# Second expert layer in three f16 products, the first bias inside the gelu, and the second layer two blocks behind the first

## What is computed

```python
x = x + attention(layernorm(x), Wq, bq, Wk, bk)        # x [4, 512, 128]
n = layernorm(x)
gate = softmax(n @ w_gate.T)                           # 8 experts
h = gelu(einsum('td,edh->teh', n, W1) + b1)            # W1 [8, 128, 512]
y = einsum('teh,ehd->ted', h, W2) + b2                 # W2 [8, 512, 128]
x = x + einsum('td..', y, top2(gate))                  # two of eight per token
```

## Time and profile before

| | |
|---|---|
| median of 3 runs | 401.67 us (398.6 to 402.32) |
| profiled execution, its own time | 401.8 us |
| its span | 400.1 us |
| TensorE busy | 338.6 us (85%) |
| ScalarE busy | 247.6 us (62%) |
| VectorE busy | 231.2 us (58%) |
| GpSimd busy | 143.0 us (36%) |
| mean granted TensorE clock | 0.978 |
| weights of a block, `wblk<-wpk` x46 | 288.0 KB, 2.7 us to landing |
| slots of a group, `xg<-xs` x10 | 260.0 KB, 3.4 us to landing |

### The profile page before, as it was taken

The page is one execution under the profiler, slowest core; times in us unless marked ns, Lnnn a source line. Parts: engine busy times, 40 slices in busy tenths (PEclk is TensorE's granted clock), DMA queues, the critical chain, the costliest instruction groups (busy, mean ns, idle before and its releaser), DMA issues.

```text
span 400.1 us, 7419 instructions
## 1 busy us (share of the span) xinstructions
PE 338.6 (85%) x2522; PEld 176.3 (44%) x2522; DVE 231.2 (58%) x619; ACT 247.6 (62%) x342; POOL 143.0 (36%) x159
## 2 busy tenths in 40 slices
PE   6777888899978989989989899999889997999900
PEld 2511333323323333323323233235779986998900
DVE  5497788677867987877789987853150000001304
ACT  1407779989878975659875768688464543444400
POOL 4994213211027017013006211036237744453450
PEclk9999999999999999999999999999899999999975
DMA  5979001100001101000201420001345754678214
GB/s 144 326 194 214 12 0 29 26 2 0 28 1 27 29 0 55 0 2 0 53 1 40 153 94 2 0 15 70 116 153 195 241 210 143 215 240 295 82 48 155
DMA packets 32863, 36.11 MB, mean 90 GB/s; under 512 B 3090, under 2 KB 23642, under 8 KB 32828
## 3 DMA queue, kind: packets, MB, share of 16 engines
q1 hardware_dynamic: 30332, 30.49, 25.9%
q0 software_dynamic: 2496, 5.15, 3.9%
HBM read 10.71 MB, written 9.25 MB: 50 GB/s over the span
## 4 chain that ended last, share of the span: by engine, by line
PE 48%; DVE 24%; ACT 9%; issue 7%; DMA 6%; POOL 3%; SPq 1%; POOLq 0%; DVEq 0%; ACTq 0%
DVE q_aug L862 13%; PE AV L1246 10%; PE SM L1199 9%; PE ST L1319 8%; PE ST L1234 6%; DMA xg<-xs 3%; ACT probs L760 2%; DVE q_aug L869 2%; PE ST L1298 2%; PE ST L1303 2%; PE ST L1301 2%; PE ST L1302 2%; DVE stats L816 2%; ACT xn L636 2%; POOL xs L529 2%
## 5 line engine op out<-in xcount | busy, mean ns | idle before, releaser
L862 DVE TENSOR_REDUCE q_aug<-SM 128x1 f16<-128x512 f32 x240 | 153.4, 688 | 46.2 <-PE SM L1199 45.2
L760 ACT ACTIVATE probs<-ST 128x1024 f32<-128x1024 f32 x128 | 125.5, 1022 | 37.3 <-PE ST L1234 36.9
L1199 PE MATMUL SM<-kTm,qT 128*128 128x512 f16 x240 | 84.0, 388 | 15.2 <-DVE q_aug L862 10.0
L1234 PE MATMUL ST<-qT,kTm 128*128 128x512 f16 x256 | 76.2, 383 | 5.0 <-ACT qT L642 4.9
L1246 PE MATMUL AV<-probs,v_aug 128*32 128x512 f32 x512 | 68.2, 605 | 3.1 <-ACT avs L752 2.9
L1199 PEld LDWEIGHTS SM<-kTm,qT 128*128 128x128 f16 x240 | 19.8, 97 | 96.0 <-DVE q_aug L862 86.3
L529 POOL DMA_INDIRECT xs<-x2s,pos x32 | 31.6, 986 | 79.5 <-DVE pos L975 70.9
L539 POOL DMA_INDIRECT yt<-w,dest x46 | 44.8, 973 | 37.5 <-ACT w L673 25.9
L665 ACT ACTIVATE w<-ST 128x512 f32<-128x512 f32 x46 | 27.3, 596 | 48.0 <-PE ST L1303 45.4
L1319 PE MATMUL ST<-w 128*128 x368 | 51.9, 285 | 1.3 <-ACT w L665 1.3
L1319 PEld LDWEIGHTS ST<-w 128*128 128x128 f32 x368 | 45.6, 195 | 1.6 <-issue 1.5
(11 more groups left out here) (174 smaller groups left out, 389.8 us busy)
## 6 DMA issues: line engine op xcount, KB each, us to landing
wblk<-wpk SPq DMA_DIRECT2D x46, 288.0 KB, 2.7
xg<-xs SPq DMA_DIRECT2D x10, 260.0 KB, 3.4
...
```

The lines of the kernel that those rows point to most:

```text
L760: act.activation(probs[:, n % 4, :, :], ST[:, n % 2, :, :], ACT.Exp, scale=SCALE).then_inc(exp_done, 1)
L862: dve.tensor_reduce(q_aug[:, b % 2, m % 4, m // 4, 24:25], SM[m % 2][:, :], AX.X, ALU.max, negate=True).then_inc(sm_max, 1)
L1199: pe.matmul(SM[m % 2][:, :], qT0[:, b % 2, h // 4, P * (m % 4):P * (m % 4) + P], kTm[:, b % 2, h // 4, h % 4, :], start=True, stop=True).t ...
L1234: mm = pe.matmul(ST[:, n % 2, k % 2, :], kTm[:, b % 2, g, k, P * c:P * c + P], qT1[:, g % 2, :], start=True, stop=True)
```

## The change

The second layer's products become f16. W2, scaled by 64, is split into a high part and a rest (`w2pk`) by eight pairs of ScalarE instructions and eight of GpSimd in batches 1 and 2, slots 12 to 15. W2 is loaded from DRAM in batch 1 into the memory of `w1`, instead of at the start into a tile of its own. The hidden values are split per block on VectorE (`split_hidden`: `hh`, `hl`, three buffers each), and `hf` has two buffers. `down` makes 12 f16 products of 128 columns (high by high, high by rest, rest by high) in place of four f32 ones; `take_y` divides by 64. The bias product with `sel` is gone: b1 is loaded as 32 rows beside the gate's, transposed with them, and stored in f32 behind each expert's weights, so a ring entry has 258 KB in place of 288. The gelu reads it as a per-partition bias, in four pieces of 128 columns. So a ring entry is free when the gelu has read it, and `fetch_weights` waits for `gelu_done`. The copy of `xgT` moves from ScalarE to VectorE. LAG is 2, and the router's steps of batch 3 are spread over steps 1 to 10.

```diff
-    WB = 2 * F + P
-    HR = 3
+    WB = 2 * F + 2 * HC
-        LAG = 1
+        LAG = 2
-            jobs = {0: [("out", b, 3)], 2: [("x2", b)], 3: [("lg", b)], 4: [("rk", b)]}.get(i, [])
+            jobs = {0: [("out", b, 3)], 4: [("x2", b)], 6: [("lg", b)], 8: [("rk", b)]}.get(i, [])
...
                 if v >= RW:
-                    sp.wait_ge(up_full, v - RW + 1)
+                    sp.wait_ge(gelu_done, v - RW + 1)
...
             for b in range(B):
                 if b == 1:
+                    sp.wait_ge(s_wl, E)
+                    sp.dma_start(w1[:, :, :].rearrange("p e (c d) -> p e c d", c=HC),
+                                 W2.rearrange("e (c p) d -> p e c d", p=P)).then_inc(s_wf[1], 16)
                     sp.wait_ge(x1_done, G)
...
+            def rest_w2(i):
+
+                pool.wait_ge(s_vh, i + 1)
+                pool.tensor_tensor(w2pk[:, i, F:2 * F], w1[:, i, :], w2pk[:, i, 0:F], ALU.subtract).then_inc(s_vl, 1)
...
             def gelu(v):
 
+                if v == 0:
+                    act.wait_ge(s_vl, E)
                 act.wait_ge(up_full, v + 1)
-                if v >= HR:
-                    act.wait_ge(down_done, v - HR + 1)
-                act.activation(hf[:, v % HR, :], UP[v % 2], ACT.Gelu, scale=1.0 / WSCALE).then_inc(gelu_done, 1)
+                if v >= 2:
+                    act.wait_ge(split_done, v - 1)
+                for c in range(HC):
+                    cs = slice(P * c, P * c + P)
+                    last = act.activation(hf[:, v % 2, cs], UP[v % 2][:, cs], ACT.Gelu, scale=1.0 / WSCALE,
+                                          bias=wblk32[:, v % RW, F + c:F + c + 1])
+                last.then_inc(gelu_done, 1)
...
+            def split_w2(e):
+
+                act.wait_ge(s_wf[1], 16)
+                act.activation(w1[:, e, :], w1[:, e, :], ACT.Copy, scale=WSCALE).then_inc(s_vfs, 1)
+                act.wait_ge(s_vfs, e + 1)
+                act.activation(w2pk[:, e, 0:F], w1[:, e, :], ACT.Copy).then_inc(s_vh, 1)
...
+            def split_hidden(v):
+
+                dve.wait_ge(gelu_done, v + 1)
+                if v >= 3:
+                    dve.wait_ge(down_done, v - 2)
+                link(dve.tensor_copy(hh[:, v % 3, :], hf[:, v % 2, :]))
+                dve.tensor_tensor(hl[:, v % 3, :], hf[:, v % 2, :], hh[:, v % 3, :], ALU.subtract).then_inc(split_done, 1)
...
                     for job in misc_of_step(b, i):
                         empty_misc(job)
-                    if i == 0:
+                    for v in todo[i:i + 1]:
+                        split_hidden(v)
+                    if i == 1:
                         second_stats(b)
...
                 dst, wb = UP[v % 2], wblk[:, v % RW, :]
-                pe.matmul(dst, wb[:, 2 * F:WB], sel[:, :, :].rearrange("p c n -> p (c n)"), start=True, stop=False)
...
-                pe.wait_ge(gelu_done, v + 1)
+                pe.wait_ge(split_done, v + 1)
+                wv = w2pk[:, bass.ds(expert[v], 1), :].rearrange("p a n -> p (a n)")
                 for c in range(HC):
-                    last = pe.matmul(dst, hf[:, v % HR, P * c:P * c + P],
-                                     w2[:, bass.ds(expert[v], 1), P * c:P * c + P].rearrange("p a n -> p (a n)"),
-                                     start=False, stop=(c == HC - 1))
+                    hi, lo = slice(P * c, P * c + P), slice(F + P * c, F + P * c + P)
+                    pe.matmul(dst, hh[:, v % 3, hi], wv[:, hi], start=False, stop=False)
+                    pe.matmul(dst, hh[:, v % 3, hi], wv[:, lo], start=False, stop=False)
+                    last = pe.matmul(dst, hl[:, v % 3, hi], wv[:, hi], start=False, stop=(c == HC - 1))
                 last.then_inc(down_done, 1)
```

117 lines of the change are left out of this document (58 added, 59 removed).

## The result

The changed kernel takes 422.3 us (median of four runs, 420.9 to 423.1) beside 401.5 for the kernel before on the same chip, a ratio of 1.0525 with a 95% interval of 1.0481 to 1.057. A second job gave 422.6 and 1.0556 (1.0500 to 1.0613). The prediction was 412 (398 to 424): the direction and the range held, the amount was half of the 20.8 us measured.

What follows compares the result with a forecast made beforehand. The slots' load loop, not TensorE, was taken to become the bound. 401.8 us plus middle 3.8, tail 3.5, start 2 and clock 1.5, less attention 0.5, gave 412 us, range 398 to 424.

Steps and rivals of the forecast that it cites:

- the attention's term: Attention of the four batches: bias splits go, W2 splits arrive on ScalarE; -0.5 us (-2 to +2).
- TensorE's price of a block, 1.38 us: Expert blocks: cheaper products cut TensorE's 1.89 us to 1.38, saving 23 us over 46 blocks if TensorE stayed the bound.
- The second rival (419): GpSimd and VectorE collide: each split loses 0.5 us to sends, 419 us; chance 0.13 together with register moves.
- The dynamic slices bring nine register moves: Second layer on TensorE: nine register moves instead of five, priced at nothing; high bound 0.6 us a block.
- The fourth rival (419): Register moves pace the second layer's products, 0.6 us more each, 419 us; chance 0.13 together with the collision.
- The slots' loop binds: Middle: the loop through the slots' load becomes the bound; cheaper products only lengthen TensorE's wait for slots.
- The turn of 8.8: Middle: one turn of the slots' loop per group takes 8.8 us (7.8 to 11.0), against 8.26 before.
- Start +2: First expert blocks: router arithmetic on VectorE stands between splits, top-2 waits for a split; +2 us (-3 to +5).
- Tail +3.5: After the last slots' landing: splits of blocks 40 to 45 queue behind the finishes; +3.5 us (+1 to +6).
- Clock +1.5: Behind TensorE's longer waits some products run at the lower clock; +1.5 us (0 to +4).
- the third rival (424, 1.2 GHz in the middle): TensorE runs the middle at half clock, the loop's products double, +1.8 us a group, 424 us; chance 0.10.
- what would show the forecast right: Slots' issues 8.2 to 9.2 us apart, TensorE waiting 1.5 to 3 every group, second layers 0.7, finish in the chain.

Runs made afterwards that it cites:

- the four edits: Changed kernel with slots loaded two steps earlier, blocks named in batch 3, expert read ahead of the second layer, finishes last: 406.8 us; also without read and moves, 395.2.

## Why the prediction was right in direction and half in size

Two steps failed. The larger is the attention's term; the other is TensorE's price of a block, 1.38 us. That 422.3 us lies inside 398 to 424 is luck: the upper end of the range was there for a slow clock.

**The attention, -0.5 (bounds -2 to +2)**, missed most: +5.4, over half of what the forecast lacked. I had priced ScalarE's new splits of W2 and left out GpSimd's eight subtractions. The second rival (419) had the mechanism, a VectorE instruction and GpSimd on one lock, but looked for it between splits and sends. There it is small: a send takes 0.97 us in most rows, a split 1.15. It sat where GpSimd computes 4.5 us in a row. With the naming moved, the term is -1.2 and inside its bounds.

**"A block then costs 1.89 - 0.51 = 1.38 us"** failed by the read of the expert number. The prediction has nothing for it but "0.11 to the next first layer", the distance at which a first layer follows the long f32 products; behind the short ones TensorE stands 0.56 to 0.66 us in most blocks and 0.82 in the turn shown. A block is 1.97 us of TensorE, more than the 1.89 before, and the saving of 23 us was never there. "The dynamic slices bring nine register moves ... I take nothing" was right for the second layers of a burst (0.67 us) and wrong by 0.2 in the loop's turn; the moves show in every block only once the read stands ahead of them. The fourth rival (419) named the moves, with 0.6 a second layer, and not the read. The run with the four edits and neither read nor moves shows 11.7 us for both. The argument against that rival, five moves in 0.95 us without a gap, was no evidence: the f32 products, 0.24 us each, covered them then.

**The slots' loop binds.** Right for the direction, and shown in part: loads two steps earlier take 7.1 us out of the 24 blocks. But TensorE was to wait 1.5 to 3 us for slots at every group's transposes, and did so at two of seven; at its real pace of 1.97 us a block it was nearly as long as the loop itself. The turn of 8.8 was sized nearly right (8.89 in the turn shown) by errors that cancel. The products are 0.89 us for 0.66, the way to the next first layer 0.82 for 0.11, that layer 0.98 for 0.86: 1.06 too little. The load (3.07 for 3.6), the gelus (1.06 for 1.26) and the way to the issue (1.27 for 1.5) were 0.96 too much. The mean of 9.31 comes from turns with longer parts, above all one of 11.41: its load was issued at 330.31 and landed at 335.61 (5.3 us), and the first layer behind it ran at the lower clock. The middle between third and last issue is +7.4, forecast +3.8. A version without the split loses 5.7 us in blocks 16 to 40 as well, so the later issue of the slots, which the prediction had, may be most of the middle's loss; no run has it alone.

**Start +2**: +3.8 in blocks 0 to 16 (+2.6 between the first gelu and the third issue, which is the prediction's cut), by VectorE, as its bounds allowed; "neither binds, but the serial pieces do" fits, since one subtraction less per split gives 4.2 back. **Tail +3.5**: +6.3 by the prediction's cut (3.9 and 2.4 by mine). Its own lines give 15.7 - 12.7 = 3.0, and no reason for 3.5. From the last landing (380.99) to the end of the last copy of results (399.77) 18.8 us pass, not 15.7. The finishes' 4 us were right (3.4 to 4.1 come back); the last send starts 5.9 us behind the copy instead of 5.1, where up to 1 us was to come back; and the lag's 1.8 at the end was not priced. **Clock +1.5** (0 to +4): the granted clock is 0.82 from 290 to 306 us, 0.96 from 306 to 322 and 0.58 from 338 to 342, and 1.00 in all three before. Set against the earlier trace rows (0.72 over 6 us) that is at most 16 x 0.18 + 16 x 0.04 + 4 x 0.42 - 6 x 0.28 = 3.5 us, an estimate. So the third rival (424, 1.2 GHz in the middle) happened in one turn of seven, and the clock between third and last issue is 0.97. Its number was nearest to the measured one by other causes.

Of what would show the forecast right, the finish in the chain came; loads 8.2 to 9.2 us apart came as 8.5 to 11.4; second layers of 0.7 us came in bursts, and as 0.8 to 1.0 behind a wait; the waits for slots at every group did not come.
